# Cross attention of a decoder: residual added in place, store ahead of the residual load, score banks freed one by one

## The chip, the cores and the metric
The kernel runs on one core of a Trainium2 chip. The metric is the time on the device in microseconds (us), of one launch that computes two whole decoder layers. The time given is the median of the runs.

## What is computed
Two decoder layers on x of shape (8, 256, 512): self attention, cross attention and a feed-forward part in each, and behind each part a residual addition and a normalization of the rows. The change touches the cross attention of the second layer alone. Its reference:

```python
def _L1_xattn_ref(q, k, v, gamma):      # q: x, k and v: the context
    N_HEAD = 8
    ...
    qh = q.reshape(B, h, dq, Lq)
    kh = k.reshape(B, h, dq, Lk)
    vh = v.reshape(B, h, dv, Lk)
    scale = 1.0 / jnp.sqrt(jnp.asarray(dq, dtype=q.dtype))
    qk = jnp.einsum('bhdq,bhdl->bhql', qh, kh) * scale
    sm = jax.nn.softmax(qk, axis=-1)
    ret = jnp.einsum('bhql,bhdl->bhdq', sm, vh)
    return gamma * ret.reshape(B, Dv, Lq)

def _layernorm(x, axis=-1, eps=1e-05):
    m = jnp.mean(x, axis=axis, keepdims=True)
    v = jnp.var(x, axis=axis, keepdims=True)
    return (x - m) / jnp.sqrt(v + eps)
```

The attention runs over the 512 features as positions: for each batch 8 heads of 32 channels, each with a 512 x 512 score matrix. The result is added to x and each row of the sum is normalized.

## The kernel before
The kernel is written for the engines directly: every engine has its own instruction stream, and semaphores order them. The stage is `l1_cross` (from L2060 on). It handles the 8 batches (numbered 0 to 7) one after the other. Each batch is 16 steps (`STEPS`; `HALF` is 8): step m covers two of the four 128-row blocks of the scores of head m // 2. Steps 0 to 7 belong to tile t = 0 of the output (4 heads, 128 of the 256 rows), steps 8 to 15 to tile t = 1. Body b is the loop round that computes the scores of batch b; the end of batch b - 1 is done inside it.

In a step, TensorE makes two score matmuls (L2346) into a pair of PSUM banks `s_ps[m % 2]`. VectorE takes the negative row maxima of both banks (L2270). ScalarE makes one exponential for each bank (L2224), with the sum of each row read out behind it. TensorE turns the result with 2 x 4 transposes (L2356) into the banks `t_ps`, two steps behind the scores; ScalarE copies one bank out (L2232), VectorE the other (L2277). In every second step TensorE adds 8 value matmuls (L2380) into the bank `v_ps`, of which there is one for all tiles. The semaphore `e_done` counts the exponentials, two in each step.

When a tile is complete, VectorE takes the reciprocals of its sums (L2282, in step 1 for the second tile of the batch before and in step 9 for the first tile of this one), TensorE spreads them over the channels (L2365), and ScalarE copies them into `rb` (L2237). `scale_out`, in steps 1 and 9 of VectorE, multiplies `v_ps` by `rb` (L2288, counted by `o_scaled`) and adds the residual from `xr` into `norm.r` (L2293, counted by `o_done`). In step 1 (t = 0) it waits first that the residual of the batch is loaded and that the store of the batch before has left `norm.r`. `finish` (step 10) takes the statistics, GpSimd computes the factor (L231, L233), and `norm.apply` (step 12) normalizes `norm.r` in place (L239). There is one `norm.r`, but there are two buffers `xr`.

For the next batch, ScalarE rounds the context and x in steps 0 and 1 (L2207), GpSimd subtracts the rounded part from each (L2132, `e_cl` and `e_xl`, both on SBUF operands), and SyncE then copies the parts into the stacked operands `qs` and `ks` with 32 transfers of 128 KB (`stack`, L2150). SyncE issues all transfers of the stage, in the order of its own stream: in body b the stack of batch b + 1, then (bodies 0 to 4, once the context of b + 1 is turned, in step 14) the loads of x and context for batch b + 3 (L2138, L2139), then the residual of batch b + 1 into `xr` (L2155), then the store of batch b - 1 (L249).

Of the kernel before, what the change touches and what calls it, by code (L numbers as in the profile page):

```python
# [14 lines left out]
P = 128  # L15
B, S, D = 8, 256, 512
T = S // P
# [6 lines left out]
ALU = mybir.AluOpType  # L24
# [28 lines left out]
def ints(x):  # L53
    return isinstance(x, int)
# [7 lines left out]
def wait_from(eng, sem, value):  # L62

    if not (ints(value) and value <= 0):
        eng.wait_ge(sem, value)
# [130 lines left out]
class Norm:  # L196

    def __init__(self, core, ctx, name, dst):  # L200
        nc = core.nc
        self.core, self.dst = core, dst
        sb = lambda n, s: ctx.enter_context(nc.sbuf_tensor(f"{name}_{n}", s, F32))
        self.r = sb("r", [P, T, D])
        self.stats = sb("stats", [P, T, 6])
        self.mv = sb("mv", [P, T, 2])
        self.rstd = sb("rstd", [P, T])
        self.added = core.sem(f"{name}_added")
        self.stats_done = core.sem(f"{name}_stats_done")
        self.stats_seen = core.sem(f"{name}_stats_seen")  # L210
        self.mv_done = core.sem(f"{name}_mv_done")
        self.eps_added = core.sem(f"{name}_eps_added")
        self.rstd_done = core.sem(f"{name}_rstd_done")
        self.y_done = core.sem(f"{name}_y_done")
        self.stored = core.sem(f"{name}_stored")
# [1844 lines left out]
def l1_cross(core, ahead, after, first_batch, x, ctx_in, y):  # L2060
    nc = core.nc
    with ExitStack() as ctx:
        sb = lambda n, s, dt=F32: ctx.enter_context(nc.sbuf_tensor(n, s, dt))
        pb = lambda n, s: ctx.enter_context(nc.psum_tensor(n, s, F32))
        sb("e_place", [P, first_batch.size // 4])
        norm = Norm(core, ctx, "n5", y)
        xs = [core.x0, sb("e_x1", [P, T, D])]
        xr = [sb(f"e_xr{u}", [P, T, D]) for u in range(2)]
        cs = [ahead.buf(0), sb("e_c1", [P, T, D])]
# [64 lines left out]
        with nc.Block() as block:  # L2134
            @block.sync
            def _(sp):
                def load(b, u):
                    sp.dma_start(xs[u][:], rows(x, b)).then_inc(x_loaded[u], 16)  # L2138
                    sp.dma_start(cs[u][:], rows(ctx_in, b)).then_inc(c_loaded[u], 16)  # L2139

                def stack(b, u):


                    sp.wait_ge(xl_done, b + 1)
                    sp.wait_ge(cl_done, b + 1)
                    for j in range(HT):
                        for dst, hi, lo, plan in ((qs, "xh", "xl", "hlhl"), (ks, "ch", "cl", "hhll")):
                            for r, part in enumerate(plan):
                                src = parts[hi if part == "h" else lo]
                                sp.dma_start(dst[u][r * CX:(r + 1) * CX, :, j, :].bitcast(F32),  # L2150
                                             src[j * CX:(j + 1) * CX, :, :].bitcast(F32)).then_inc(stacked[j], 16)

                def residual(b, u):
                    wait_from(sp, o_done, T * (b - 1))
                    sp.dma_start(xr[u][:], rows(x, b)).then_inc(r_loaded[u], 16)  # L2155

                load(1, 1)
                residual(0, 0)
                sp.wait_ge(c_turned, 2)
                load(2, 0)  # L2160

                def body(b, u, more):
                    if not (ints(b) and b == B - 1):
                        stack(b + 1, 1 - u)
                    if more:
                        sp.wait_ge(c_turned, 2 * b + 4)
                        load(b + 3, 1 - u)
                    if not (ints(b) and b == B - 1):
                        residual(b + 1, 1 - u)
                    if not (ints(b) and b == 0):  # L2170
                        norm.store(sp, b - 1)
                for b in range(B):
                    body(b, b % 2, b < B - 3)
                after.load_x(sp)
                norm.store(sp, B - 1)
                sp.wait_ge(norm.stored, 16 * B)

            @block.gpsimd
# [85 lines left out]
            @block.vector  # L2264
            def _(dve):
                def maxima(b, m):
                    n, i = STEPS * b + m, m % 2
                    dve.wait_ge(s_mm, n + 1)
                    wait_from(dve, e_done, 2 * (n - 1))
                    dve.tensor_reduce(nb[i][:], s_ps[i][:], AX.X, ALU.max, negate=True).then_inc(nb_done, 1)  # L2270

                def copy_t(b, m):
                    n, j, q = STEPS * b + m, m // 2 % HT, 2 * (m % 2) + 1
                    t = m // (HALF)
                    dve.wait_ge(t_mm, 2 * n + 2)
                    wait_from(dve, v_mm, T * b + t - 1)
                    dve.tensor_copy(pT[t][:, j, :, q * P:(q + 1) * P], t_ps[1][:]).then_inc(td_done, 1)  # L2277

                def reciprocals(b, t):
                    dve.wait_ge(e_done, 2 * (STEPS * b + HALF * (t + 1)))  # L2280
                    wait_from(dve, r_mm, T * b + t - 1)
                    dve.reciprocal(rs[t][:], sums[t][:]).then_inc(rs_done, 1)  # L2282

                def scale_out(b, u, t):

                    dve.wait_ge(v_mm, T * b + t + 1)
                    dve.wait_ge(m_read, m_count(b, t))
                    dve.tensor_tensor(rb[:], v_ps[:], rb[:], ALU.mult).then_inc(o_scaled, 1)  # L2288
                    dve.wait_ge(o_scaled, T * b + t + 1)
                    if t == 0:  # L2290
                        in_buffer(dve, r_loaded, b, u)
                        norm.wait_stored(dve, b)
                    dve.tensor_tensor(norm.r[:, t, :], xr[u][:, t, :], rb[:], ALU.add).then_inc(o_done, 1)  # L2293

                def finish(b, u):
                    norm.statistics(dve, b, [(o_done, T * b + t + 1) for t in range(T)])

                def body(b, u, first, last):
                    for m in range(STEPS):
                        maxima(b, m)  # L2300
                        for c, r in before(b, m, first):
                            copy_t(c, r)
                            if r == STEPS - 1 or r == HALF - 1:
                                reciprocals(c, r // (HALF))
                        if m in (1, HALF + 1) and not first:
                            scale_out(b - 1, 1 - u, m // HALF)
                        if m == HALF + 2 and not first:
                            finish(b - 1, 1 - u)
                        if m == HALF + 4 and not first:
                            norm.apply(dve, b - 1)  # L2310

                def tail(b, u):
                    copy_t(b - 1, STEPS - 2)
                    scale_out(b - 1, 1 - u, 0)
                    copy_t(b - 1, STEPS - 1)
                    reciprocals(b - 1, 1)
                    scale_out(b - 1, 1 - u, 1)
                    finish(b - 1, 1 - u)
                    norm.apply(dve, b - 1)
                over_batches(dve, body, tail)  # L2320

            @block.tensor
            def _(pe):
# [16 lines left out]

                def scores(b, u, m):
                    n, i, h = STEPS * b + m, m % 2, m // 2
                    wait_from(pe, e_done, 2 * (n - 1))
                    for a in range(2):
                        q = 2 * (m % 2) + a
                        last = pe.matmul(s_ps[i][:, a, :], qs[u][:, h // HT, h % HT, q * P:(q + 1) * P],  # L2346
                                         ks[u][:, h // HT, h % HT, :], start=True, stop=True)
                    last.then_inc(s_mm, 1)
# [21 lines left out]
                def values(b, u, t, part):  # L2370

                    if part == 0:
                        n = STEPS * b + HALF * (t + 1)
                        pe.wait_ge(ta_done, n)
                        pe.wait_ge(td_done, n)
                        wait_from(pe, o_done, T * b + t)
                    start = sum(per_part[:part])
                    for k, j in [divmod(n, HT) for n in range(start, start + per_part[part])]:
                        e = t * P + j * CX
                        last = pe.matmul(v_ps[j * CX:(j + 1) * CX, :], vt[u][:, k, e:e + CX], pT[t][:, j, k, :],  # L2380
                                         start=(k == 0), stop=(k == LB - 1), skip_group_check=True,
                                         tile_position=(0, j * CX))
                    if part == PARTS - 1:
                        last.then_inc(v_mm, 1)
# [371 lines left out]
```

## Time and profile before

| | us |
|---|---|
| median of 3 runs | 2036.05 |
| lowest, highest | 2035.22, 2041.91 |
| profiled execution: its span | 2041.2 |
| cross attention in it | from about 1600 to 1950 |

| engine | busy us | share of the span |
|---|---|---|
| TensorE, matmuls (PE) | 1832.9 | 90% |
| TensorE, loads of weights (PEld) | 1493.2 | 73% |
| VectorE (DVE) | 1253.9 | 61% |
| ScalarE (ACT) | 918.1 | 45% |
| GpSimd (POOL) | 290.8 | 14% |

The profile records one execution. All its times count from the start of the span. "Idle before <- X" beside an instruction says how long its engine had nothing to do before it and what released it; a releaser is inferred from the semaphores. SPq is the queue of SyncE, whose instructions are issues of transfers. The granted clock of TensorE is given in parts of full speed (2.4 GHz).

### The profile page before, as it was taken

How to read it: one execution, taken by the hardware profiler on the slowest of the kernel's cores; microseconds unless marked ns; L12 is line 12 of the kernel's file. 1: busy time of each engine (PE TensorE's matmuls, PEld its weight loads, DVE VectorE, ACT ScalarE, POOL GpSimd, SP SyncE). 2: the span in 40 equal slices, each digit the busy share in tenths (PEclk: the TensorE clock that was granted, in tenths of full speed). 3: DMA queues.
4: the chain of work that ended last, by engine and by line, in shares of the span. 5: the costliest groups of instructions: out<-in, count | busy, mean ns of one | idle time of the engine just before them, and what ended most of it. 6: DMA issues, size and time to landing. Idle time of an engine off the chain costs nothing. (4 is left out here: it accounts for less than half of the span.)

```text
span 2041.2 us, 33020 instructions
## 1 busy us (share of the span) xinstructions
PE 1832.9 (90%) x12272; PEld 1493.2 (73%) x12272; DVE 1253.9 (61%) x2330; ACT 918.1 (45%) x2376; POOL 290.8 (14%) x347
## 2 busy tenths in 40 slices
PE   6979999999997889999999987899997698889966
PEld 5868999999885778888888885677775455555543
DVE  3446444444447656555654536788887587778847
ACT  2225333333334443333333214676666587778811
POOL 0000000000012111111111001333334112111001
PEclk9989999999999999999999998999997899899988
DMA  3022000000014221101110013000013575665134
GB/s 106 32 95 92 21 22 22 22 21 1 22 53 129 83 73 42 47 19 40 48 37 17 11 42 124 12 32 32 32 53 96 148 170 147 151 150 127 49 118 142
DMA packets 86253, 136.62 MB, mean 67 GB/s; under 512 B 9480, under 2 KB 25480, under 8 KB 86096
## 3 DMA queue, kind: packets, MB, share of 16 engines
q1 hardware_dynamic: 86096, 134.52, 23.2%
q8 instruction: 99, 1.62, 0.3%
q14 instruction: 58, 0.48, 0.1%
HBM read 79.88 MB, written 21.05 MB: 49 GB/s over the span
## 5 line engine op out<-in xcount | busy, mean ns | idle before, releaser
L2224 ACT ACTIVATE e_p<-e_s_ps,e_nb 128x512 f32<-128x512 f32 x256 | 175.1, 698 | 45.5 <-DVE e_nb L2270 43.7
L2270 DVE TENSOR_REDUCE e_nb<-e_s_ps 128x2 f32<-128x1024 f32 x128 | 155.8, 1218 | 51.2 <-PE e_s_ps L2346 50.5
L1710 ACT ACTIVATE p<-p,nb,rq 128x128 f32<-128x128 f32 (+1 forms) x256 | 136.9, 541 | 92.9 <-DVE nb L1811 92.9
L2356 PE MATMUL e_t_ps<-ident,e_p 128*128 128x128 f32 x1024 | 147.7, 283 | 21.2 <-DVE e_pT L2277 13.5
L894 PE MATMUL yp<-ccy,toep 128*128 128x288 f32 x600 | 159.1, 413 | 5.7 <-ACT ccy L876 3.6
L2356 PEld LDWEIGHTS e_t_ps<-ident,e_p 128*128 128x128 f32 x1024 | 120.1, 146 | 58.9 <-issue 49.6
L80 PE MATMUL q_ps<-a_xt_hi,wq_hi 128*128 128x256 f32 x512 | 151.3, 296 | 4.1 <-DVE wo_lo L112 4.1
L1231 DVE SCALAR_TENSOR_TENSOR hm<-gu_ps,us_col,sg 128x256 f32<-128x256 f32 x88 | 42.3, 481 | 177.4 <-ACT sg L1120 177.4
L82 PE MATMUL q_ps<-a_xt_hi,wq_lo 128*128 128x256 f32 x512 | 145.7, 285 | 0.0
L81 PE MATMUL q_ps<-a_xt_lo,wq_hi 128*128 128x256 f32 x512 | 145.4, 284 | 0.0
L527 ACT ACTIVATE ex<-ex 128x512 f32<-128x512 f32 x64 | 40.4, 632 | 213.1 <-DVE ex L590 213.1
L894 PEld LDWEIGHTS yp<-ccy,toep 128*128 128x128 f32 x600 | 111.1, 193 | 34.2 <-ACT ccy L876 8.1
L231 POOL TENSOR_TENSOR n_rstd<-n_mv,eps 128x2 f32<-128x2 f32 x32 | 6.3, 195 | 856.8 <-DVE n_mv L225 856.8
L1120 ACT ACTIVATE sg<-gu_ps,gs_col 128x256 f32<-128x256 f32 x88 | 41.6, 473 | 187.6 <-PE gu_ps L82 187.6
L568 DVE TENSOR_TENSOR tl<-t_ps,th 128x512 fp32r<-128x512 f32 x64 | 44.3, 692 | 132.4 <-ACT th L519 132.4
L1663 POOL TENSOR_TENSOR p<-p,rs 128x512 f32<-128x512 f32 x64 | 94.1, 1470 | 188.6 <-DVE rs L1818 188.6
L80 PE MATMUL gu_ps<-m_xt_hi,wg_hi 128*128 128x256 f32 x352 | 101.2, 287 | 11.9 <-DVE m_xt_lo L1223 8.2
L80 PE MATMUL o_ps<-wo_hi,th 128*128 128x512 f32 x256 | 106.6, 416 | 1.5 <-DVE tl L568 1.5
L590 DVE TENSOR_SCALAR ex<-q_ps,bq_col 128x256 f32<-128x256 f32 x128 | 55.8, 478 | 79.2 <-PE q_ps L82 79.2
L80 PEld LDWEIGHTS q_ps<-a_xt_hi,wq_hi 128*128 128x128 f32 x512 | 98.3, 192 | 4.6 <-issue 4.5
L81 PE MATMUL o_ps<-wo_lo,th 128*128 128x512 f32 x256 | 101.2, 395 | 0.0
L82 PE MATMUL o_ps<-wo_hi,tl 128*128 128x512 f32 x256 | 101.1, 395 | 0.0
(300 smaller groups left out, 5151.7 us busy)
## 6 DMA issues: line engine op xcount, KB each, us to landing
x_after<-n_r SPq DMA_DIRECT2D x24, 512.0 KB, 3.0
toep<-padded_kernels SPq DMA_DIRECT2D x32, 256.0 KB, 3.6
qs<-e_xh SPq DMA_DIRECT2D x64, 128.0 KB, 2.5
qs<-e_xl SPq DMA_DIRECT2D x64, 128.0 KB, 2.6
ks<-e_ch SPq DMA_DIRECT2D x64, 128.0 KB, 2.6
ks<-e_cl SPq DMA_DIRECT2D x64, 128.0 KB, 2.7
x<-x_after SPq DMA_DIRECT2D x12, 512.0 KB, 4.5
x<-in_x SPq DMA_DIRECT2D x8, 512.0 KB, 4.0
```

Source lines behind the costliest of these rows:

```text
L80: pe.matmul(out, whi, xhi, start=start, stop=False)
L81: pe.matmul(out, whi, xlo, start=False, stop=False)
L82: return pe.matmul(out, wlo, xhi, start=False, stop=stop)
L568: dve.tensor_tensor(tl[:], t_ps[:], th[:], ALU.subtract).then_inc(tl_done, 1)
L590: dve.tensor_scalar(ex[p % 2][:, h, :], q_ps[p % 2][:, h, :], bq_col[:, head:head + 1], 0.0, ALU.add, ALU.min).then_inc(mq_done, 1)
L894: last = pe.matmul(yp[:, lo % 2, 0:NCOL], self.toep[h % 2][:, (lo - li) * P:(lo - li + 1) * P], self.ccy(h)[:, li, 0:NCOL], start=(li == 0 ...
L1231: dve.scalar_tensor_tensor(hm[:], gu_ps[n % 2][:, 1, :], us_col[:, j:j + 1], sg[:], ALU.mult, ALU.mult).then_inc(hm_done, 1)
L1663: pool.tensor_tensor(tile, tile, r, ALU.mult).then_inc(pn_done, 1)
L1710: act.activation(p[n % 3][:, h, part[t]], p[n % 3][:, h, part[t]], ACT.Exp, bias=nb[i][:, t, h:h + 1], scale=rq[u][:, t:t + 1], accum_out= ...
L2224: act.activation(pr[i][:, a, :], s_ps[i][:, a, :], ACT.Exp, bias=nb[i][:, a:a + 1], accum_out=sums[t][:, j, q:q + 1]).then_inc(e_done, 1)
L2270: dve.tensor_reduce(nb[i][:], s_ps[i][:], AX.X, ALU.max, negate=True).then_inc(nb_done, 1)
L2356: last = pe.transpose(t_ps[a][:, k, :], pr[m % 2][:, a, k * P:(k + 1) * P], core.ident[:])
```

## The change
Five edits, all for the cross attention. The class `Norm` can be made without its own buffer `r`, and here it is: sum, statistics, normalization and store work on the residual's own buffer `xr[u]`. VectorE's wait for the store is gone from `scale_out`. SyncE stores batch b - 1 before it loads the residual of batch b + 1 into the same buffer, and waits for the landing of that store in between. The first value matmul of a tile waits for `o_scaled` (the multiplication) instead of `o_done` (the addition). The first of the two score matmuls of a step waits for the first exponential of two steps ago, the second for the second.

```diff
-    def __init__(self, core, ctx, name, dst):
+    def __init__(self, core, ctx, name, dst, own=True):
...
-        self.r = sb("r", [P, T, D])
+        self.r = sb("r", [P, T, D]) if own else None
...
-        norm = Norm(core, ctx, "n5", y)
+        norm = Norm(core, ctx, "n5", y, own=False)
...
                 def residual(b, u):
-                    wait_from(sp, o_done, T * (b - 1))
+                    norm.wait_stored(sp, b - 1)
                     sp.dma_start(xr[u][:], rows(x, b)).then_inc(r_loaded[u], 16)
...
+                    if not (ints(b) and b == 0):
+                        norm.store(sp, b - 1, r=xr[1 - u])
                     if not (ints(b) and b == B - 1):
                         residual(b + 1, 1 - u)
-                    if not (ints(b) and b == 0):
-                        norm.store(sp, b - 1)
                 for b in range(B):
                     body(b, b % 2, b < B - 3)
                 after.load_x(sp)
-                norm.store(sp, B - 1)
+                norm.store(sp, B - 1, r=xr[(B - 1) % 2])
...
                     if t == 0:
                         in_buffer(dve, r_loaded, b, u)
-                        norm.wait_stored(dve, b)
-                    dve.tensor_tensor(norm.r[:, t, :], xr[u][:, t, :], rb[:], ALU.add).then_inc(o_done, 1)
+                    dve.tensor_tensor(xr[u][:, t, :], xr[u][:, t, :], rb[:], ALU.add).then_inc(o_done, 1)
...
-                    norm.statistics(dve, b, [(o_done, T * b + t + 1) for t in range(T)])
+                    norm.statistics(dve, b, [(o_done, T * b + t + 1) for t in range(T)], r=xr[u])
...
-                            norm.apply(dve, b - 1)
+                            norm.apply(dve, b - 1, r=xr[1 - u])
...
                 def scores(b, u, m):
                     n, i, h = STEPS * b + m, m % 2, m // 2
-                    wait_from(pe, e_done, 2 * (n - 1))
                     for a in range(2):
+                        wait_from(pe, e_done, 2 * (n - 2) + a + 1)
                         q = 2 * (m % 2) + a
...
-                        wait_from(pe, o_done, T * b + t)
+                        wait_from(pe, o_scaled, T * b + t)
```

## Rows read from the trace of the kernel before

**Rows 1.** The page, its head.
```profile
span 2041.2 us, 33020 instructions
```
**Rows 2.** Who waited for whom, 1600 to 1950 us: total us, times, longest.
```profile
PE e_v_ps L2380 <- DVE n_r L2293: 13.7, 6, 3.2
DVE n_r L2293 <- DMA x_after<-n_r: 10.9, 4, 3.8
...
PE e_s_ps L2346 <- ACT e_p L2224: 3.2, 7, 2.0
```
**Rows 3.** Stretches: bodies 1, 2, 5, 6 between reciprocals; then 6 us of body 2.
```profile
core 0: us, PE busy (x) PEld busy (x) DVE busy (x) ACT busy (x) POOL busy (x), PEclk, DMA share, GB/s
1644.44:1664.37 19.93, 18.15 (x148) 11.37 (x148) 17.50 (x20) 18.11 (x45) 4.76 (x2) 1.00 0.77 190
1684.49:1708.77 24.28, 20.63 (x148) 13.14 (x148) 15.88 (x20) 17.41 (x43) 4.24 (x2) 0.86 0.81 194
...
1817.60:1841.86 24.26, 20.67 (x148) 13.19 (x148) 17.91 (x20) 17.41 (x43) 4.25 (x2) 0.86 0.76 176
1861.99:1880.96 18.97, 18.14 (x148) 11.38 (x148) 16.54 (x21) 17.13 (x43) 4.29 (x2) 1.00 0.61 130
...
1690.00:1696.00 6.00, 6.00 (x24) 3.74 (x24) 3.82 (x5) 3.27 (x8) 0.00 (x0) 0.50 0.88 189
```
**Rows 4.** Timeline of body 2: start, us, engine, line, count, idle before and releaser.
```profile
1684.01 2.37 POOL L2132 TENSOR_TENSOR e_cl<-e_c,e_ch 128x1024 fp32r<-128x1024 f32 x1 [11.91 <-ACT e_ch L2207]
...
1684.65 0.63 DVE L2288 TENSOR_TENSOR e_rb<-e_v_ps,e_rb 128x512 f32<-128x512 f32 x1
...
1686.78 2.34 POOL L2132 TENSOR_TENSOR e_xl<-e_x,e_xh 128x1024 fp32r<-128x1024 f32 x1 [0.40 <-ACT e_xh L2207]
1689.05 0.69 DVE L2293 TENSOR_TENSOR n_r<-e_xr,e_rb 128x512 f32<-128x512 f32 x1 [3.78 <-DMA x_after<-n_r]
1689.15 0.59 SPq L2150 DMA_DIRECT2D qs<-e_xh  x1
...
1689.89 1.93 PE L2380 MATMUL e_v_ps<-e_pT,e_vt 128*32 128x512 f32 x8 [3.25 <-DVE n_r L2293]
```
**Rows 5.** The same timeline, the add of body 3.
```profile
1731.54 2.54 DVE L2293 TENSOR_TENSOR n_r<-e_xr,e_rb 128x512 f32<-128x512 f32 x1 [1.85 <-DMA x_after<-n_r]
```
**Rows 6.** The same timeline, the same place of body 6.
```profile
1861.51 2.38 POOL L2132 TENSOR_TENSOR e_cl<-e_c,e_ch 128x1024 fp32r<-128x1024 f32 x1 [11.91 <-ACT e_ch L2207]
...
1862.81 1.63 DVE L2293 TENSOR_TENSOR n_r<-e_xr,e_rb 128x512 f32<-128x512 f32 x1
...
1864.58 1.07 PE L2380 MATMUL e_v_ps<-e_pT,e_vt 128*32 128x512 f32 x8 [0.45 <-DVE n_r L2293]
```
**Rows 7.** Store of 1676 to 1692 us, its KB and landing; SyncE's last stack issues.
```profile
x_after<-n_r SPq DMA_DIRECT2D x1, 512.0 KB, 8.5
...
1680.42 0.47 SPq L249 DMA_DIRECT2D x_after<-n_r  x1
...
1708.53 1.24 SPq L2150 DMA_DIRECT2D ks<-e_cl  x2
```
**Rows 8.** Timeline of two steps of the steady part.
```profile
1677.72 0.70 PE L2346 MATMUL e_s_ps<-ks,qs 128*128 128x512 f32 x2
...
1678.46 1.23 DVE L2270 TENSOR_REDUCE e_nb<-e_s_ps 128x2 f32<-128x1024 f32 x1 [1.14 <-PE e_s_ps L2346]
...
1680.43 0.63 PE L2356 MATMUL e_t_ps<-ident,e_p 128*128 128x128 f32 x4 [0.16 <-DVE e_pT L2277]
...
1681.98 0.73 PE L2346 MATMUL e_s_ps<-ks,qs 128*128 128x512 f32 x2
```
**Rows 9.** Weight loads: of two transpose groups, of one; of the scores (ns min/median/max).
```profile
1623.53 0.86 PEld L2356 LDWEIGHTS e_t_ps<-ident,e_p 128*128 128x128 f32 x8 [0.25 <-issue]
...
1680.40 0.42 PEld L2356 LDWEIGHTS e_t_ps<-ident,e_p 128*128 128x128 f32 x4 [0.37 <-issue]
...
L2346 PEld LDWEIGHTS e_s_ps<-ks,qs x256: 186/190/338, 1603.2 to 1931.9; 128*128 128x128 f32 x128
```

More of the change, by code:

```diff
@@ L2318, in tail @@
                     finish(b - 1, 1 - u)
-                    norm.apply(dve, b - 1)
+                    norm.apply(dve, b - 1, r=xr[1 - u])
                 over_batches(dve, body, tail)
```

## Prediction
> **What bounds the kernel now.** The change lies in one stage, the cross attention. I read the page first for the span (2041.2 us [rows 1]), then the waits of the stage alone, from 1600 to 1950 us. Two of them form a pair: TensorE waits 13.7 us in 6 places for the residual add, and VectorE, in front of that add, waits 10.9 us in 4 places for a store to DRAM [rows 2]. The third row there is the wait at which the new score condition aims: TensorE idles only 3.2 us in 7 places before its score matmuls because of an exponential [rows 2]. Then I cut the stage at the reciprocals of VectorE (one in step 1 and one in step 9 of each body of 16 steps) and compared first halves, each with the same TensorE work. The first halves of bodies 2 to 5 take 24.28, 24.24, 24.24 and 24.26 us (the first and the last of the four stand in [rows 3]); those of bodies 1 and 6, which find the store landed or need none, take 19.93 and 18.97 [rows 3]. Two things are in the difference. TensorE stands still for 3.25 us before its value matmuls, and then runs for 6 us at a granted clock of 0.50, the lower level of 1.2 GHz, so that the same 8 value matmuls take 1.93 us instead of 1.07 [rows 3, 4, 6]. The granted clock of a whole long first half is 0.86, of body 6 it is 1.00 [rows 3]. So the bound at these places is neither a busy engine nor a transfer that work needs: it is a buffer that must be empty before the next sum may be written into it.
>
> What ends the stall needs one more look. In body 2 the add begins at 1689.05 and takes 0.69, in body 3 it begins 1.85 us after its turn and then takes 2.54, and both halves are equally long within 0.04 [rows 3, 4, 5]. The store landed almost 2 us earlier in body 3 and nothing was won: the add (two operands in SBUF) came to its end only after GpSimd's second subtraction, which ends at 1689.12 in body 2 [rows 4]. In body 6 the add starts under the first subtraction (1861.51 to 1863.89) and ends at 1864.44, at 1.63 us instead of 0.69 [rows 6]: it slips into the 0.4 us between GpSimd's two instructions.
>
> **The change, part by part.** (1) The sum is written into the loaded residual buffer, and VectorE's wait for the store of the batch before is gone. In body 2 the add would then start at 1685.3, when the multiplication ends, 1.3 us into GpSimd's first subtraction (1684.01 to 1686.38) [rows 4]. That is the state of body 6, where it starts 1.3 us into it as well [rows 6]. So I price each of the bodies 2 to 5 by body 6: 24.28 + 24.24 + 24.24 + 24.26 = 97.02, less 4 x 18.97 = 75.88, gives 21.1 us. That contains the stall of TensorE and the return to the full clock. What is late next in these places is GpSimd's subtraction, already inside the 18.97. The bodies 1, 6 and 7 and the last batch gain nothing from this part. No row shows a first half with both subtractions in it that is shorter than body 6's, so 21.1 is the upper bound; the lower is body 1's 19.93: 97.02 - 79.72 = 17.3 us [rows 3].
>
> The Trainium skill (SBUF — State Buffer, "Who interferes with whom") says that a VectorE instruction with two SBUF inputs and a GpSimd instruction that reads SBUF exclude each other for a whole instruction, whichever starts first. This trace agrees, with the 2.54 us of body 3's add [rows 5]. The add keeps both operands in SBUF, so by that rule the change cannot make the add free, and if GpSimd's second subtraction took the port first, most of the stall would stay; that is the first rival below, priced there from rows.
>
> (2) The order on SyncE. Before: two loads for three batches ahead, the residual load, the store. Now the store comes ahead of the residual load, which waits until that store has landed. The store took 8.5 us to land from 1680.42, behind three loads [rows 7]; the 32 copies of the stack for the next batch are queued behind the waiting SyncE. They could start only at 1689.15 anyway, when GpSimd's second subtraction was done [rows 4]. Taking 8.5 us again from a place one issue earlier (about 1679.9) the store lands at 1688.4, and the residual load is issued by 1688.9: no delay, and at worst about 1 us. The last pair of stack copies is issued at 1708.53 [rows 7], at the end of the first half, with eight steps to go before the next body needs the first of them: cover of some 17 us at two steps in 4.26 us [rows 8]. The residual now arrives about a body before it is read. Cost 0; with the cover gone it would be the 1 us in each of 4 bodies.
>
> (3) The value matmuls wait for the multiplication that empties their PSUM bank, no longer for the add behind it. In bodies 1 to 6 TensorE would no longer idle there; in body 6 that is 0.45 us [rows 6]. But VectorE, which must deliver the next maximum, is held by the add as before, so little of it passes on. Bounds 0 and 6 x 0.45 = 2.7 us; I take 0.2 each, 1.2 us, nearer to nothing, because the maximum of body 6 stands right behind the add and not behind TensorE.
>
> (4) A score bank is free after its own exponential, one earlier than before (0.7 us). In the steady part the chain is: score matmuls at 1677.72 (0.70), maximum at 1678.46, VectorE's copy behind it, second half of the transposes at 1680.43 (released by that copy), value matmuls, next score matmuls at 1681.98 [rows 8]. It has a period of 4.26 us for two steps and the exponential is not in it, so the earlier bank gives nothing there. It gives something where TensorE really waits for one: 3.2 us in 7 places, the longest of 2.0 in the first steps of batch 0 [rows 2]. In most of the others ScalarE is itself without a gap and nothing is won. I take 0.5 us, bounds 0 and 3.2. The edit adds one wait per step, 128 in all, between the two score matmuls. Where both waits of a pair of transposes are fulfilled, 8 weight loads take 0.86 us, the same spacing as 4 in 0.42 [rows 9]: a fulfilled wait costs nothing that these rows show. I take 0. The upper bound is the load of weights made visible, 0.19 us each [rows 9], 24.3 us.
>
> (5) The 4 KB buffer per partition that is not allocated costs and brings nothing by itself.
>
> **Sum.** 21.1 + 1.2 + 0.5 = 22.8 us. The profiled execution took about its span, 2041.2, with 0.7 around it if it is the run of 2041.91; less 22.8 it gives 2019.1. It is 5.9 us above the median of 2036.05, and against that median the forecast is **2013.2 us**, a ratio of 0.989.
>
> **The rivals.** *The gap is missed* (chance 0.06): without the store wait the add still loses to GpSimd's second subtraction and ends at 1689.7 as now. For it: in bodies 2 and 3 it did end there [rows 4, 5]. Against: it had started after the first subtraction was over, and in body 6 it had not [rows 6]. TensorE would have done its value matmuls before, and only some 1.6 us of stall and about 1 us of slow clock would go: 4 x 2.6 = 10.4, so 2025.7 us.
>
> *Most of the stall is the profiler's* (0.08): the 5.9 us between the profiled run and the median lie in just these stalls. Then 22.8 - 5.9 = 16.9, so 2019.2. Against: the halves last alike although the store landed 2 us apart [rows 3 to 5].
>
> *The new wait keeps the second weight load from running ahead* (0.04): 128 x 0.19 = 24.3 us in the very chain that sets the period, so 2037.5, no change.
>
> *The new wait costs more than that, and the kernel is slower* (0.04): between the two score matmuls come the load of 0.19 and a start like the 0.16 us that TensorE idles behind a release of VectorE [rows 8, 9]. 128 x 0.35 = 44.8, so 2058. It decides from 22.8 / 128 = 0.18 us per step on.
>
> *More passes on* (0.08): all 2.7 us of part 3 and all 3.2 of part 4: 21.1 + 5.9 = 27.0, so 2009.
>
> **How the numbers follow.** My forecast has 0.70: 2013.2, by itself between 2011 and 2017 (body 1 as the model instead of body 6 costs 3.8 us). The range for 8 in 10 takes in the two neighbouring cases and 1 us for the spread of medians, 2008 to 2020; the missed gap and both costs of the new wait stay outside (0.14). 0.3% is 6.1 us, about what a measurement of this kernel can tell from no change. Faster by more: 0.70 + 0.08 + 0.08 + 0.05 of the missed gap = 0.91. Same: 0.04 + 0.01 = 0.05. Slower: 0.04.
>
> **What the changed profile would show.** Right: no wait of VectorE for a store in this stage and no wait of TensorE for the add; first halves of bodies 2 to 5 of 18.7 to 19 us at a granted clock of 1.00; the add starting under GpSimd's first subtraction and ending about 0.5 us after it; score matmuls still two in 0.70 to 0.73; the steady period still 4.26. Wrong: an add that ends after the second subtraction; a pair of score matmuls longer than 0.73 in the steady part; score matmuls that wait for the stack copies; second halves that grow.

## The result, and the profile after

The changed kernel takes 2016.47 us (median of 4 runs, 2013.69 to 2018.77), the kernel before 2035.63 (4 runs). The ratio is 0.9898 with a 95% interval of 0.9879 to 0.9917. The profiled execution has a span of 2013.2 us. Five further runs gave a median of 2014.76, against 2035.36 in nine of the kernel before (0.9897, 0.9874 to 0.9919).

The stretches of the kernel after, cut at the same reciprocals as before: the first halves of bodies 1, 2, 5 and 6, and the second half of body 1 (columns as in [rows 3]):

```profile
core 0: us, PE busy (x) PEld busy (x) DVE busy (x) ACT busy (x) POOL busy (x), PEclk, DMA share, GB/s
1641.11:1660.97 19.86, 18.17 (x148) 11.45 (x148) 17.53 (x20) 18.09 (x45) 4.78 (x2) 1.00 0.76 188
1660.97:1681.09 20.12, 17.79 (x149) 11.32 (x148) 17.85 (x27) 17.24 (x45) 3.22 (x4) 1.00 0.59 148
1681.09:1699.86 18.77, 18.15 (x148) 11.45 (x148) 16.45 (x21) 17.01 (x43) 4.29 (x2) 1.00 0.74 178
...
1836.69:1855.46 18.77, 18.14 (x148) 11.45 (x148) 16.45 (x21) 17.02 (x43) 4.28 (x2) 1.00 0.58 127
```

The five first halves of bodies 2 to 6 take 18.77 to 18.79 us, where four of them took 24.24 to 24.28 and the fifth 18.97 [rows 3]. The granted clock is 1.00 in all of them. The place where body 2 stood still [rows 4] now looks like this in the timeline (start, us, engine):

```profile
1680.61 2.38 POOL L2132 TENSOR_TENSOR e_cl<-e_c,e_ch 128x1024 fp32r<-128x1024 f32 x1 [11.91 <-ACT e_ch L2207]
...
1681.24 0.63 DVE L2288 TENSOR_TENSOR e_rb<-e_v_ps,e_rb 128x512 f32<-128x512 f32 x1
...
1681.91 1.63 DVE L2292 TENSOR_TENSOR e_xr<-e_xr,e_rb 128x512 f32<-128x512 f32 x1
...
1682.71 0.36 SPq L2155 DMA_DIRECT2D e_xr<-x_after  x1
...
1683.06 1.04 PE L2379 MATMUL e_v_ps<-e_pT,e_vt 128*32 128x512 f32 x8
...
1683.38 2.39 POOL L2132 TENSOR_TENSOR e_xl<-e_x,e_xh 128x1024 fp32r<-128x1024 f32 x1 [0.40 <-ACT e_xh L2207]
...
1685.80 0.59 SPq L2150 DMA_DIRECT2D qs<-e_xh  x1
```

The add starts right behind the multiplication, under GpSimd's first subtraction, and ends at 1683.54, 0.55 us after it: what body 6 did before [rows 6]. The value matmuls follow the spreading of the sums without a wait. SyncE has the residual load out at 1682.71, 3.1 us before the stack could begin. The landings of that stretch (KB, us from issue to landing):

```profile
x_after<-e_xr SPq DMA_DIRECT2D x1, 512.0 KB, 6.5
e_xr<-x_after SPq DMA_DIRECT2D x1, 512.0 KB, 3.6
```

One thing differs that the change did not do. The end of the stage, from the last reciprocal to the last multiplication, is 4.88 us after and was 6.56 before, for the same 64 matmuls. These are the two stretches, before and then after:

```profile
1937.94:1944.50 6.56, 6.20 (x64) 2.69 (x64) 0.24 (x2) 0.69 (x1) 0.00 (x0) 0.74 0.00 0
```
```profile
1912.42:1917.30 4.88, 4.51 (x64) 1.81 (x64) 0.24 (x2) 0.69 (x1) 0.00 (x0) 1.00 0.00 0
```

The granted clock was 0.74 there before and 1.00 after. From the last reciprocal to the first statistics behind it, every profiled kernel of this document took either 7.9 us or 6.2, and both values stand with the old waits and with the new ones, so I count these 1.7 us as chance. That is argued and not shown: no kernel was seen with both values.

### The profile page after: what moved, and what is told of

Same layout as the page of the kernel before. It is cut to its first block and busy times, and to the rows that moved or that the text cites. A ratio compares the mean times of both kernels' runs of the same rounds, so it can differ in the third digit from the quotient of the medians.

```text
span 2013.2 us, 33020 instructions
## 1 busy us (share of the span) xinstructions
PE 1816.6 (90%) x12272; PEld 1484.4 (74%) x12272; DVE 1251.9 (62%) x2330; ACT 916.3 (46%) x2376; POOL 290.7 (14%) x347
## 5 line engine op out<-in xcount | busy, mean ns | idle before, releaser
L2355 PEld LDWEIGHTS e_t_ps<-ident,e_p 128*128 128x128 f32 x1024 | 115.2, 142 | 62.7 <-issue 53.2
```

What stands on the lines that cost most here:

```text
L2355: last = pe.transpose(t_ps[a][:, k, :], pr[m % 2][:, a, k * P:(k + 1) * P], core.ident[:])
```

## The experiments

"First half" and "second half" are the stretches between the reciprocals throughout. Behind body 1, and at a granted clock of 1.00, they repeat within 0.03 us where nothing differs (one half of one kernel, named below, is an exception). So they tell more than the time of the whole kernel, whose single runs scatter over 3 to 12 us in one comparison.

**The sum in place alone.** The change without its two new waits of TensorE:

```diff
-                    for a in range(2):
-                        wait_from(pe, e_done, 2 * (n - 2) + a + 1)
+                    wait_from(pe, e_done, 2 * (n - 1))
+                    for a in range(2):
...
-                        wait_from(pe, o_scaled, T * b + t)
+                        wait_from(pe, o_done, T * b + t)
```

> The changed kernel with the old waits put back: the value matmuls wait for the add, the two score matmuls of a step wait together. What is left of the change is the sum in place and the store ahead of the residual load. My theory: all of the stall goes with this part. First halves of bodies 2 to 6 of 18.97 us as body 6 had before, granted clock 1.00 in them, body 1 at 19.93; the whole kernel about 2 us behind the changed one (1.0 of the value wait in six bodies, 0.5 to 1 in the first steps). Rival, the waits of TensorE carry the gain: first halves of bodies 2 to 5 stay above 22 us.

Bodies 2 and 6 in it:

```profile
1685.44:1704.42 18.98, 18.14 (x148) 11.37 (x148) 16.55 (x20) 17.16 (x43) 4.32 (x2) 1.00 0.72 170
...
1841.87:1860.84 18.97, 18.13 (x148) 11.38 (x148) 16.54 (x20) 17.16 (x43) 4.29 (x2) 1.00 0.62 132
```

18.97 or 18.98 in all five, 2017.62 us for the kernel (0.9901, 0.9868 to 0.9934). The whole stall goes with this part, and the model "body 6" holds to 0.01 us. The two waits of TensorE together bring the remaining 0.2 us per body; they were not tried one by one. By the medians this kernel is 1.2 us behind the changed one, by the stage 1.4, where about 2 were expected. Body 1 took 20.16, not 19.93; why was not followed up.

**The two waits of TensorE alone**, on the kernel before.

> The kernel before with the two new waits of TensorE alone (value matmuls wait for the multiplication, each score matmul for its own exponential); the sum still goes into its own buffer and waits for the store. My theory: the add still ends after GpSimd's second subtraction, so the first halves of bodies 2 to 5 lose only what TensorE can do ahead, its value matmuls: 24.25 becomes 21.5 to 23 us, since the stall before the value matmuls (3.2 us) is cut in two and the clock may stay up. Whole kernel 5 to 11 us faster than before. Rival, the value wait is what stalls the stage: first halves fall to 19 us. Rival, the waits give nothing: 24.2 us.

2032.28 us (0.9979, 0.9962 to 0.9996). Bodies 2 to 5:

```profile
1685.47:1707.02 21.55, 18.15 (x148) 11.44 (x148) 16.83 (x20) 17.05 (x43) 4.29 (x2) 1.00 0.78 189
1727.14:1750.24 23.10, 19.64 (x148) 12.14 (x148) 17.24 (x20) 17.23 (x43) 4.28 (x2) 0.93 0.77 181
1770.38:1794.30 23.92, 20.24 (x148) 12.76 (x148) 15.79 (x20) 17.40 (x43) 4.28 (x2) 0.86 0.77 183
1814.44:1836.79 22.35, 18.97 (x148) 12.46 (x148) 17.96 (x21) 17.30 (x43) 4.28 (x2) 0.92 0.75 174
```

The expectation held for two bodies of the four; one was above it (23.92) and one just above (23.10). The stall is not cut in two, as I had expected: TensorE makes its value matmuls and goes on, then stands still in one place for 2.97 to 3.28 us, for VectorE's copy that comes behind the add. The four bodies are alike but for body 4, whose add ends 0.3 us later, and what differs with their length is the column PEclk: the one at 1.00 takes 21.55, the others are 0.8 to 2.4 us longer at 0.86 to 0.93. The stage became 6.6 us shorter; the medians show 4.3 us (0.8 to 7.7 by the interval), where 5 to 11 were expected. Only a small part is to be had by these waits while the store is still waited for.

**The store first**, nothing in place: one move on SyncE in the kernel before.

```diff
+                    if not (ints(b) and b == 0):
+                        norm.store(sp, b - 1)
                     if more:
                         sp.wait_ge(c_turned, 2 * b + 4)
                         load(b + 3, 1 - u)
                     if not (ints(b) and b == B - 1):
                         residual(b + 1, 1 - u)
-                    if not (ints(b) and b == 0):
-                        norm.store(sp, b - 1)
```

> The kernel before, with one move on the queue of SyncE: the store of batch b - 1 stands ahead of the wait for the turned context and of the two loads. The sum keeps its own buffer, VectorE still waits for the store. My theory: the store is then issued after step 12 and lands in 3 to 4 us, before step 1 of the next body, so the wait is met and the stall goes without any edit of buffers: first halves of bodies 2 to 5 of 18.97 us, kernel as fast as the one with the sum in place (within 1 us in this stage). Rival, the shared buffer itself costs: first halves of 20 us and more.

Body 2, and the store of that stretch:

```profile
1683.55:1702.50 18.95, 18.14 (x148) 11.38 (x148) 16.52 (x20) 17.13 (x43) 4.28 (x2) 1.00 0.64 141
...
1672.63 0.37 SPq L249 DMA_DIRECT2D x_after<-n_r  x1
...
x_after<-n_r SPq DMA_DIRECT2D x1, 512.0 KB, 2.8
```

First halves of 18.95 to 18.98, 2018.44 us (0.9914, 0.9883 to 0.9945). Issued as soon as the rows are normalized, the store lands in 2.8 us instead of 8.5 [rows 7], long before the next body, and the wait in front of the add is met. So the stall was one of order on a queue; another buffer was not what was missing. The move does two things at once, which were not tried apart. The store no longer stands behind SyncE's wait for the turned context (step 14): it is issued 10.9 us ahead of the reciprocal of step 1 instead of 4.1. And it no longer shares the way with three loads, so it lands 5.7 us faster. By these numbers, an estimate, either alone would have had it landed before the add's turn, 0.8 us behind the reciprocal.

**No store, but the gap missed.** The changed kernel, whose add waits for ScalarE's second rounding:

```diff
                         in_buffer(dve, r_loaded, b, u)
+                        if b + 2 < B:
+                            dve.wait_ge(xh_done, b + 3)
                     dve.tensor_tensor(xr[u][:, t, :], xr[u][:, t, :], rb[:], ALU.add).then_inc(o_done, 1)
```

> The changed kernel, in which no engine waits for a store before the add; instead the add of step 1 waits for ScalarE's second rounding (which is what starts GpSimd's second subtraction), for as long as there is a next batch to round. My theory, that the stall of the kernel before was as long as it was because the add missed the gap between GpSimd's two subtractions: the adds of bodies 1 to 6 end only after the second subtraction, 2.3 us long or more instead of 0.69, without any store in play. The first halves come back to 22 to 24 us, like those of the kernel before with the new waits alone (21.55 to 23.92). Rival, the landing of the store alone set the length: the add runs its 0.7 us as soon as the rounding is done, and the first halves take 20 us at most.

Body 2 in the timeline, then the first halves of bodies 2 to 5:

```profile
1686.07 2.37 POOL L2132 TENSOR_TENSOR e_xl<-e_x,e_xh 128x1024 fp32r<-128x1024 f32 x1 [0.39 <-ACT e_xh L2207]
1686.12 2.86 DVE L2294 TENSOR_TENSOR e_xr<-e_xr,e_rb 128x512 f32<-128x512 f32 x1 [1.56 <-ACT e_xh L2207]
```
```profile
1683.77:1705.31 21.54, 18.16 (x148) 11.44 (x148) 17.68 (x21) 17.03 (x43) 4.27 (x2) 1.00 0.75 171
1725.44:1748.55 23.11, 19.65 (x148) 12.13 (x148) 17.77 (x21) 17.21 (x43) 4.26 (x2) 0.93 0.77 175
1768.67:1792.46 23.79, 20.39 (x148) 12.93 (x148) 17.96 (x20) 17.39 (x43) 4.28 (x2) 0.86 0.75 171
1812.58:1835.02 22.44, 19.06 (x148) 12.56 (x148) 17.95 (x20) 17.29 (x43) 4.28 (x2) 0.92 0.76 173
```

The add starts 0.05 us behind the subtraction, takes 2.86 us (0.69 alone) and ends 0.54 us after it. Without any store in play the halves come out as with the store and the same waits of TensorE: 21.54, 23.11, 23.79, 22.44 against 21.55, 23.10, 23.92, 22.35 (the first just below what was expected). Bodies 1 and 6, which had no stall before, take 23.30 and 23.11 here. One run gave 2037.46 us: all of the gain gone. The rival of the missed gap is a real mechanism; the change just does not run into it.

**TensorE kept busy through the stall**: the kernel before, in which the 32 small matmuls that spread the sums are made four times over in bodies 2 to 5.

```diff
-                    for q in range(NQ):
+                    for q in [q for _ in range(4 if t == 1 and 1 <= b <= 4 else 1) for q in range(NQ)]:
```

> The kernel before, in which TensorE does the spreading of the sums of bodies 2 to 5 four times over at step 2 (96 small matmuls more for each, same values, same bank), so that it is busy during the stall instead of idle. My theory, that about 1.5 us of the 5.3 us per body is the return to the full clock: granted clock 1.00 in the 6 us behind the stall (0.50 before), value matmuls at 1.07 instead of 1.93 us, first halves of bodies 2 to 5 of 22 to 23 us instead of 24.25, though the kernel does more. Rival, the clock does not matter because other engines set the pace: 24.2 us as before, with the clock up.

Its body 2, and the 6 us behind the stall:

```profile
1683.91:1705.66 21.75, 20.77 (x244) 13.99 (x244) 16.32 (x20) 17.15 (x43) 4.28 (x2) 1.00 0.76 184
```
```profile
1689.00:1695.00 6.00, 5.71 (x38) 3.11 (x39) 5.42 (x7) 4.63 (x12) 0.00 (x0) 1.00 0.80 172
```

21.73 to 21.75 us in all four, with a clock of 1.00 where it was 0.50 [rows 3], and 2030.43 us for the kernel in one run. The add ends 5.2 us behind the reciprocal, as in the kernel before, so the stall is the same; with 96 matmuls more per body the half is 2.5 us shorter. So of the 5.3 us per body 2.5 are the clock and 2.8 the stall itself. I had put the clock at 1.5, and the halves are shorter than the 22 to 23 expected.

**Many waits.** The changed kernel with the wait in front of each score matmul written five times; 504 instructions more are in the profile (33524 for 33020).

> The changed kernel with the wait in front of each score matmul written five times (four more for each of 256 matmuls, all fulfilled when the first is). My theory, that a fulfilled wait costs TensorE nothing visible: steady period of two steps 4.29 us as before, first halves 18.8 us, second halves 20.1. Rival, a wait costs TensorE's queue some time: at 0.02 us each, 16 per two steps make 4.6 us of the period and 10 to 20 us for the kernel; at 0.05 us each 40 us and more.

2018.72 us in one run, first halves of 18.76 to 18.79, second halves of 20.12 to 20.13. The score matmuls, ns min/median/max of 256, in this kernel and in the changed one:

```profile
L2346 PE MATMUL e_s_ps<-ks,qs x256: 387/472/776, 1603.2 to 1909.6; 128*128 128x512 f32 x128
```
```profile
L2345 PE MATMUL e_s_ps<-ks,qs x256: 387/475/796, 1599.8 to 1906.6; 128*128 128x512 f32 x128
```

Not all the copies of the wait show as instructions (504 of 1024), and those that do cost the halves nothing. They are not free in themselves. Where the second exponential is not yet done when TensorE comes to the second matmul of a pair, the pair is longer than 0.73 us, already in the changed kernel: some 0.91 and 0.80 in each of the first halves of bodies 1 to 6. With the copies these pairs take 1.03 and 0.97 in body 2, and a third one 0.83 instead of 0.72. The first of them in body 2, in the changed kernel and in this one:

```profile
1685.80 0.91 PE L2345 MATMUL e_s_ps<-ks,qs 128*128 128x512 f32 x2
```
```profile
1688.87 1.03 PE L2346 MATMUL e_s_ps<-ks,qs 128*128 128x512 f32 x2
```

No half became longer by it, so other work hides it here. What settles the two rivals of part 4 is the changed kernel itself: its second halves are 20.11 to 20.13 us as before, and the rivals would have made each of them 1.5 or 2.8 us longer (8 x 0.19 or 8 x 0.35).

**The change again**, in five rounds.

> The changed kernel once more, in five rounds against the kernel before. The stage itself is 22.1 us shorter by its halves, if the end of the stage is left out, where the granted clock differs by chance. My theory: the 19.2 us of the first comparison of medians is the same gain with the scatter of the rest of the kernel in it (the start of the stage alone moves between 1601.1 and 1605.8 us with the same code ahead of it); more runs give a difference of means of 20.5 to 23.5 us. Rival, the unprofiled kernel before stalls less than the profiled one: 17 to 19.5 us.

Median 2014.76 against 2035.36; the means of the 5 and of the 9 runs are 2015.2 and 2036.2, so 21.0 us. The first halves repeat: 18.77, 18.79, 18.78, 18.79, 18.77. The start of the stage, by its first maximum, lies between 1600.7 and 1606.1 us over all kernels here, with the same code ahead of it. That scatter is enough to explain why the first medians show 19.2. It does not exclude the rival: the interval of the ratio reaches from 16.5 to 25.7 us and holds both forecasts.

**The port freed.** The changed kernel with ScalarE's roundings in steps 1 and 2 in place of 0 and 1.

```diff
-                            if m == (3 if first else 0):
+                            if m == (3 if first else 1):
                                 round_hi(b + 1, 1 - u, "ch")
-                            if m == (4 if first else 1):
+                            if m == (4 if first else 2):
                                 round_hi(b + 1, 1 - u, "xh")
```

> The changed kernel with ScalarE's two roundings for the next batch one step later (steps 1 and 2 instead of 0 and 1, batch 0 as it was), so that GpSimd's first subtraction begins only when VectorE's add is over. My theory: the add of step 1 takes 0.69 us instead of 1.63 and the first halves of bodies 2 to 6 fall from 18.77 towards the 18.04 of body 7, which has no subtraction: 18.1 to 18.4 us, 2 to 4 us for the kernel. Rival, the add is hidden by other work or the roundings cost the same one step later: 18.7 us and no change. Rival, the later stack transfers make the scores of the next batch wait: slower.

The expectation failed and the first rival held. The add takes 0.69 us in every body, body 1 falls from 19.86 to 18.78, and bodies 2 to 6 stay at 18.78 to 18.80; the kernel took 2016.47. The fall of body 1 is not the add's either, for in the kernel of many waits its add took 0.69 us too and the half was 19.82; there, as in the changed kernel, TensorE waited 1.6 to 2.0 us for ScalarE's copy. What the add gave up, another wait took in the next steps:

```profile
1684.94 1.05 ACT L2207 ACTIVATE e_xh<-e_x 128x1024 fp32r<-128x1024 f32 x1
...
1685.89 0.59 ACT L2232 ACTIVATE e_pT<-e_t_ps 128x512 f32<-128x512 f32 x1
...
1686.62 1.06 PE L2355 MATMUL e_t_ps<-ident,e_p 128*128 128x128 f32 x8 [0.98 <-ACT e_pT L2232]
```

ScalarE's second rounding stands in front of its copy, and TensorE waits 0.98 us for that copy.

**The rounding in step 5** (steps 1 and 5).

> The changed kernel with ScalarE's two roundings in steps 1 and 5 (the run before had them in 1 and 2, where the add was free of GpSimd but TensorE waited 0.98 us for ScalarE's copy behind the second rounding). My theory, that the 0.73 us by which the first halves exceed body 7's 18.04 is ScalarE's copy held up by a rounding in an even step: in an odd step ScalarE has room, and the first halves of bodies 1 to 6 take 18.0 to 18.2 us, 4 to 5 us for the kernel. Rival, the 2.1 us of rounding have to be paid wherever they stand: 18.8 us again. Rival, the stack starts some 8 us later and the scores of the next batch wait for it.

18.32 to 18.34 us in bodies 1 to 6 and 2011.64 us in one run. Most of what stood above body 7's 18.03 was indeed the place of the rounding; 0.3 us is left, more than the 0 to 0.2 that I expected. No wait of the scores for the stack appears.

**Statistics split.** The same, with tile 0's statistics in step 5:

```diff
+                        if m == 5 and not first:
+                            finish(b - 1, 1 - u, 0)
                         if m == HALF + 2 and not first:
-                            finish(b - 1, 1 - u)
+                            finish(b - 1, 1 - u, 1)
```

> The same, and the statistics of tile 0 are taken in step 5, not together with those of tile 1 in step 10. My theory: TensorE's wait of 1.29 us for VectorE's copy in every second half is due to the 1.5 us of statistics in one step; with 0.6 us less in it the second halves of bodies 1 to 7 take 19.4 to 19.6 instead of 20.12, and the first halves grow by no more than 0.3: about 3 us more. Rival, the first halves grow by what the second ones lose.

TensorE's wait for VectorE's copy in the second half of body 1, in the kernel with the roundings moved and in this one:

```profile
1665.80 0.63 PE L2355 MATMUL e_t_ps<-ident,e_p 128*128 128x128 f32 x4 [1.29 <-DVE e_pT L2277]
```
```profile
1664.63 0.63 PE L2365 MATMUL e_t_ps<-ident,e_p 128*128 128x128 f32 x4 [0.70 <-DVE e_pT L2277]
```

Second halves of 19.52 or 19.53 for 20.13, first halves unchanged but for one (18.52). 2008.05 us (0.986, 0.9832 to 0.9888), faster than both kernels of the case: its slowest run, 2009.1, is below the fastest of the changed kernel, 2012.43, and its stage takes 310.9 us where the changed kernel's takes 317.1 and 317.6.

**Normalization split** over steps 12 and 13, on top.

> The same, and the normalization is spread over steps 12 and 13, one tile in each. My theory: VectorE has 0.7 us to spare in two steps, so 0.5 us in each of two steps costs less than 1.0 in one, but TensorE waits hardly for it today: 0 to 0.3 us per second half, 0 to 2 us. With both edits ahead of it the kernel is 5 to 9 us faster than the changed kernel, 2006 to 2011 us. Rival, no gain beyond the scatter.

Second halves 19.52 to 19.54, 2008.21 us (0.9863, 0.9835 to 0.989): no gain. The two tiles' normalization costs no more in one step than in two.

## Why the prediction was right, point by point

The forecast was 2013.2 us in 2008 to 2020 and the median is 2016.47. Term by term, in the profiled stage from its first maximum to its last statistics (341.4 us before, 317.6 after, 23.8 less):

| term | forecast, us | measured, us |
|---|---|---|
| stall and clock in bodies 2 to 5 (part 1) | 21.1 | 21.1 (the sum in place alone: 97.02 - 75.92) |
| value wait in bodies 1 to 6, with what the score wait does there | 1.2 | 1.1 (5 x 0.2, and 0.07 in body 1) |
| earlier bank in the first steps (part 4) | 0.5 | -0.1 (first reciprocal 0.14 earlier, the next one 0.22 later behind it) |
| SyncE's order (part 2) | 0 | 0 |
| added waits | 0 | 0 |
| end of the stage, clock 0.74 before | none | 1.7, by chance |

**Part 1 held to a tenth.** The choice of body 6 over body 1 as the model was the step that carried the number, and the reason for it, the phase of the add to GpSimd's subtraction, was shown: in bodies 2 to 6 the add begins 1.3 us into it and takes 1.63 us. The lower bound by body 1 would have given 17.3. What the prediction named as late next, GpSimd's subtraction, is not what holds the 18.77: with the add free of it the halves stayed as they were, and ScalarE's roundings were what could be moved.

**What ended the stall** was read rightly. The experiment with no store and the gap missed brings the long halves back, and the one with the store first shows that the landing is the first cause. It makes the add late, and GpSimd's second subtraction can make it later. In the kernel before, the adds of bodies 2 and 4 began 4.56 and 4.42 us behind the reciprocal, when that subtraction was all but over, and lost next to nothing to it; those of bodies 3 and 5 began 2.65 and 2.47 behind it, and took 2.54 and 2.72 us instead of 0.69. All four ended 5.18 to 5.25 behind the reciprocal. That the buffer had to be empty was true, but "in place" was not needed to empty it.

**The clock's share was not priced apart.** In the rival of the missed gap I put about 1 us per body on it. It is 2.5 of 5.3 us. That rival was thus mis-sized. With the new waits and the gap missed the halves were 21.5 to 23.8, on average 1.5 us per body less than before where I had 2.6: 2036.05 - 6.1 gives 2029.9 and not 2025.7. (The run with the gap missed took 2037.46, but it was made to miss it in bodies 1 and 6 as well, 7.5 us more by the halves.) For the forecast it made no difference, since body 6's row holds both.

**Part 2**: the store landed in 6.5 us instead of the 8.5 I carried over, and the residual load was out 3.1 us before the stack, where I had counted on 0.2. It erred to the safe side.

**Part 4** was a little too high. The kernels with the new score wait reach the first reciprocal 20.2 to 20.9 us after the first maximum, those without 21.0 to 21.6: 0.7 us gained on average. But the half behind it takes 19.14 to 19.17 with it and 18.93 to 18.95 without (19.01 in the kernel of many waits). Those 0.2 us are no work that became slower: in the changed kernel the first value matmuls come 2.01 us behind the reciprocal where they came 1.79 behind it, and all that follows keeps this distance, so only the mark moved. What is left is 0.5 us over all kernels, as forecast, and -0.1 in the two that the table compares; kernels that differ in nothing there scatter as much. In the steady part the wait brings nothing, as the chain of [rows 8] said.

**The signs of being wrong.** One of them came, a second half that grew: it is the 0.2 us of body 0, the moved mark. Another nearly came: two pairs of score matmuls in each first half of bodies 1 to 6 are longer than 0.73 us, while in the steady part of these bodies none is beyond 0.74. They cost no half any time.

**Against the median** 3.3 us are missing: 22.8 were forecast and 19.2 measured, and the kernel before came out 0.4 us faster in its four runs than in the three of the forecast. The second time it was 20.6. The stage's own gain, without its end, is 22.1. I had asked whether the profiler lengthens the stall. The 5.9 us by which the profiled run of the kernel before stood above the median are no sign of it, for the kernel with the normalization split has no stall, and its profiled run stood 6.1 us above the mean of its other three. But the runs are too few to exclude a small effect; the remainder of some 1 to 3 us is within the scatter and stays open.

## What to carry to other kernels

When an engine waits for a store, look first at where the store stands in its queue, and behind which waits. Here moving it ahead of one wait and of three loads that nobody needs for a long time was worth as much as the sum in place, within 0.5 us in the stage. Price a removed stall by a round of the same loop that does not have it, and check that the round has the same neighbours in the same phase; it then includes the clock that comes back. After that the next gains were found by asking which copy an instruction holds up in its own stream: the two roundings and one tile's statistics, moved by a few steps, brought another 7 us or so (2014.76 to 2008.05). How long a single instruction takes is no guide to that: the add went from 1.63 to 0.69 us and no half became shorter.

## What the runs showed of the hardware

A VectorE add with both operands in SBUF (0.69 us alone) took 1.63 us when it began 1.3 us into a GpSimd subtraction, and 2.86 when it began 0.05 us behind one. It ended 0.55 us after that subtraction each time. In the first case GpSimd's next subtraction, 0.4 us later, did not keep it out. The other way round it happened once, in body 1 of the kernel of many waits: the add began first and took its 0.69 us, and the subtraction that began 0.21 us behind it took 2.71 us instead of 2.37.

```profile
1644.99 0.69 DVE L2292 TENSOR_TENSOR e_xr<-e_xr,e_rb 128x512 f32<-128x512 f32 x1
...
1645.20 2.71 POOL L2132 TENSOR_TENSOR e_cl<-ring,e_ch 128x1024 fp32r<-128x1024 f32 x1 [23.72 <-ACT e_ch L2207]
```

This is the lock that the Trainium skill describes (SBUF — State Buffer, "Who interferes with whom"). The traces agree with it in both directions, but for 0.14 us at the end of the subtraction, in which the two records overlap.

The granted clock behind a stall was not the same for the same idle time. With no pause above 0.6 us in the half TensorE had 1.00; with 3.25 us of idleness it had 0.50 in the 6 us behind. Where the value matmuls went ahead and TensorE stood still for 2.97 to 2.99 us behind them (3.28 in one body), the halves of four bodies had 1.00, 0.93, 0.86 and 0.92, and two different kernels had the same four values in the same order. That agreement was not expected, and its cause is open.
